# A transformer layer on one core: projections held back behind a stack load, GpSimd for the rows of the maxima, and weighting two key tiles behind the scores

## The reference, cut to what matters

```python
h = layernorm(x) * (1 + ca) + sa                   # ca, sa, ... from silu(c) @ wmod
qkv = h @ w_qkv.T + b_qkv                          # heads of width 16
scores = q @ k.T / 4 + causal                      # per head, 2048 x 2048
x = x + ga * ((softmax(scores) @ v) @ w_out.T + b_out)
h = layernorm(x) * (1 + cb) + sb
gate = h @ gate_weight.T                           # top-1 of 8 experts, 320 places each
x = x + gb * experts(h)                            # exact gelu, scatter and gather by rank
```

## Time and profile before

| what | value |
|---|---|
| three runs, us | 782.27, 780.64, 782.81; median 782.27 |
| profiled execution, us | 778.72 |
| its span, first to last instruction, us | 777.0 |
| mean granted TensorE clock | 0.927 of 2.4 GHz |
| PE busy | 676.4 us, 87% |
| DVE busy | 561.8 us, 72% |
| ACT busy | 455.8 us, 59% |
| POOL busy | 134.1 us, 17% |

### The profile page before, as it was taken

One profiled execution on the slowest core, in us unless ns is written; L12 is line 12 of the kernel. 1 busy time (PEld: TensorE's weight loads), 2 busy tenths in 40 slices (PEclk: granted clock), 3 DMA queues, 4 the chain that ended last, 5 costly groups with the idle time before them and its releaser, 6 DMA issues.

```text
span 777.0 us, 12195 instructions
## 1 busy us (share of the span) xinstructions
PE 676.4 (87%) x4290; PEld 370.4 (48%) x4290; DVE 561.8 (72%) x1467; ACT 455.8 (59%) x962; POOL 134.1 (17%) x194
## 2 busy tenths in 40 slices
PE   4686889489899999999999999988986279999994
PEld 3555444232333344333333333334533269999994
DVE  7763778468798987989998989974435447777762
ACT  1432546256577776777777777765761346666651
POOL 6000322130001122103221101100005300121122
PEclk9988889689899999999999999999987569999997
DMA  7435236531005123106800032000004283455200
GB/s 244 105 91 136 48 75 147 127 71 23 1 1 133 31 55 82 29 1 155 280 1 1 1 122 96 2 0 28 29 27 152 106 232 116 158 193 202 81 23 18
DMA packets 42111, 66.53 MB, mean 86 GB/s; under 512 B 3822, under 2 KB 31985, under 8 KB 41466
## 3 DMA queue, kind: packets, MB, share of 16 engines
q1 hardware_dynamic: 39746, 59.44, 27.3%
q0 software_dynamic: 2304, 6.31, 2.2%
HBM read 39.36 MB, written 26.78 MB: 85 GB/s over the span
## 4 chain that ended last, share of the span: by engine, by line
PE 69%; DVE 9%; issue 8%; ACT 7%; DMA 4%; POOL 1%; SPq 1%; DVEq 0%; POOLq 0%; ACTq 0%
PE bank L1280 15%; PE bank L1330 13%; PE bank L1358 13%; PE bank L1464 9%; PE bank L1447 8%; PE bank L1225 3%; ACT probs L842 3%; DMA qk_rows<-part 2%; PE bank L1383 2%; PE bank L1430 1%; DVE chunk_max L1089 1%; PE bank L1254 1%; PE bank L1407 1%; ACT stacks L831 1%; ACT qk_sb L792 1%
## 5 line engine op out<-in xcount | busy, mean ns | idle before, releaser
L842 ACT ACTIVATE probs<-bank 128x512 f32<-128x512 f32 (+3 forms) x640 | 295.2, 540 | 105.4 <-PE bank L1358 103.6
L1089 DVE TENSOR_REDUCE chunk_max<-bank 128x1 f32<-128x512 f32 x384 | 251.5, 685 | 30.4 <-PE bank L1330 28.7
L1358 PE MATMUL bank<-stacks 104*128 104x512 bf16 (+3 forms) x640 | 188.3, 358 | 19.6 <-DVE stacks L1115 12.3
L1330 PE MATMUL bank<-stacks 96*128 96x512 bf16 (+3 forms) x640 | 195.6, 359 | 7.1 <-DVE chunk_max L1089 4.0
L1280 PE MATMUL bank<-probs,v_sb 128*32 128x512 f32 (+3 forms) x1280 | 154.8, 557 | 0.4 <-POOL probs L738 0.4
L1095 DVE CUSTOM_DVE_ANT_0 masked<-bank,causal 128x128 bf16<-128x128 f32 (+3 forms) x256 | 120.7, 484 | 21.6 <-PE bank L1330 20.6
L1330 PEld LDWEIGHTS bank<-stacks 96*128 96x128 bf16 x640 | 55.6, 98 | 154.2 <-DVE chunk_max L1089 74.6
L738 POOL TENSOR_SCALAR_AFFINE_SELECT probs<-probs 128x512 f32<-128x512 f32 x64 | 40.8, 638 | 383.9 <-ACT probs L842 383.9
L1358 PEld LDWEIGHTS bank<-stacks 104*128 104x128 bf16 x640 | 63.1, 101 | 83.4 <-ACT probs L842 18.4
L1464 PE MATMUL bank<-w_split,acts 128*128 128x256 f32 x576 | 79.3, 283 | 0.0
L1464 PEld LDWEIGHTS bank<-w_split,acts 128*128 128x128 f32 x576 | 73.9, 189 | 1.5 <-issue 0.8
(11 more groups left out here) (140 smaller groups left out, 538.2 us busy)
## 6 DMA issues: line engine op xcount, KB each, us to landing
stacks<-qk_rows SPq DMA_DIRECT2D x6, 1536.0 KB, 12.2
w_raw<-w_in SPq DMA_DIRECT2D x8, 1024.0 KB, 5.0
w_raw<-w_down SPq DMA_DIRECT2D x8, 1024.0 KB, 8.1
qk_rows<-part SPq DMA_DIRECT2D x32, 192.0 KB, 2.8
slot_rows<-empty SPq DMA_DIRECT2D x1, 5140.0 KB, 28.9
slots_sb<-slot_rows SPq DMA_DIRECT2D x8, 514.0 KB, 4.2
qk_rows<-part SPq DMA_DIRECT2D x32, 128.0 KB, 2.4
stacks<-qk_rows SPq DMA_DIRECT2D x8, 384.0 KB, 4.3
```

What stands on the lines that cost most here:

```text
L842: act.activation(probs[:, s % 3, h, 0:width], of_ring(*ev)[:, 0:width], ACT.Exp)\
L1089: dve.tensor_reduce(to, src[:, 0:QB], AX.X, ALU.max).then_inc(max_read, 1)
L1330: pe.matmul(bank[MAX_BANKS[u % 3]][:, 0:width], stack(g, 0)[0:KR, h, q0:q0 + P], stack(g, 1)[0:KR, h, c * QB:c * QB + width], start=True, ...
L1358: pe.matmul(of_ring(*ev)[:, 0:QB - lo], stack(g, 1)[0:KR + MR, h, kt * P:(kt + 1) * P], stack(g, 0)[0:KR + MR, h, b * QB + lo:(b + 1) * QB ...
```

## The change

Three edits. First, the planner holds back a group's projections while the stacks of the group before are on their way: a new condition `stacks_on_way` asks that `STACK_TIME - SPLIT_TIME` (15000 of the planner's nanoseconds) have passed since `parts_at` of the group before. Second, from block n = 4 on (`PARTS_BY_POOL`), the split of the maxima and the copy of the rows to three heads run on GpSimd instead of VectorE; `neg_max` gets two buffers and a semaphore of its own, and the planner's costs for these steps are changed. Third, a key tile is weighted two tiles behind its scores (`WEIGH_LAG`) instead of one; the turn of the heads of the block before moves from the second to the third key tile, and its `heads_out` from the first to the second.

```diff
+PARTS_BY_POOL = NB
+WEIGH_LAG = 2
...
             plan.append(("max_parts", n))
-            vector[-1] += 400
-            waiting_rows.append([n, vector[-1] + 100])
+            vector[-1] += 640 if n < PARTS_BY_POOL else 220
+            waiting_rows.append([n, vector[-1] + 100 + (0 if n < PARTS_BY_POOL else 800)])
...
-            placed_at[n] = now + 1700
-            vector[-1] = max(vector[-1], now + 550) + 450
+            placed_at[n] = now + (1700 if n < PARTS_BY_POOL else 2700)
+            if n < PARTS_BY_POOL:
+                vector[-1] = max(vector[-1], now + 850) + 690
...
-        if projections and not split and block >= PROJECT_FROM[projections[0][0]] and now >= projected + SPLIT_TIME:
+        stacks_on_way = projections and now < parts_at.get(projections[0][0] - 1, 0.0) + STACK_TIME - SPLIT_TIME
+        if projections and not split and not stacks_on_way and block >= PROJECT_FROM[projections[0][0]] \
+                and now >= projected + SPLIT_TIME:
...
-                if may_go_beside(n, (i, h) > (1, 1)) and not (n == NG * NB - 1 and h == HG - 1):
+                if may_go_beside(n, (i, h) > (WEIGH_LAG, 1)) and not (n == NG * NB - 1 and h == HG - 1):
...
-                if h == 1 and n >= 1 and i == 1:
+                if h == 1 and n >= 1 and i == WEIGH_LAG:
                     plan.append(("turn_heads", n - 1))
...
-            if weigh is not None:
+            if len(weighings) == WEIGH_LAG:
+                weigh = weighings.pop(0)
                 fill(weigh[3])
                 plan.append(("weigh", weigh[0], weigh[1]))
                 tensor(HG * weigh[2] * 234 / QB, weigh[3])
-                if weigh[0] < n:
+                if weigh[0] < n and i == WEIGH_LAG - 1:
                     plan.append(("heads_out", n - 1))
...
     plan += beside
-    plan.append(("weigh", weigh[0], weigh[1]))
+    for weigh in weighings:
+        plan.append(("weigh", weigh[0], weigh[1]))
... on GpSimd
+                if ev[0] == "max_parts" and ev[1] >= PARTS_BY_POOL:
+                    pool.wait_ge(neg_max_known, n + 1)
+                    pool.wait_ge(ring_filled, turn_of["max_rows", n - 2] + 1)
+                    link(pool.tensor_copy(max_part[:, n % 2, :, 0], neg))
+                    pool.tensor_tensor(max_part[:, n % 2, :, 1], neg, max_part[:, n % 2, :, 0], ALU.subtract)\
+                        .then_inc(max_parts, 1)
+                if ev[0] == "max_rows" and ev[1] >= PARTS_BY_POOL:
+                    pool.wait_ge(diag_done, masked_tiles)
+                    if biased:
+                        pool.wait_ge(x_biased, biased)
+                    pool.wait_ge(rest_ready_p, n_rests)
+                    if n_parts:
+                        pool.wait_ge(qk_split_p, n_parts)
+                    pool.wait_ge(max_row0, n + 1)
+                    pool.tensor_copy(rows[:, 1:HG, :], rows[:, 0:1, :].broadcast_to([MR, HG - 1, QB]))\
+                        .then_inc(max_rows, 1)
+                    pool.wait_ge(max_rows, n + 1)
... on VectorE
                     if n >= 2:
+                        dve.wait_ge(max_parts, n - 1)
+                    neg = neg_max[:, n % 2, :]
+                    dve.tensor_reduce(neg, chunk_max[:, n % 2, :, 0:b + 1], AX.X, ALU.max, negate=True)\
+                       .then_inc(neg_max_known, 1)
+                    if n < PARTS_BY_POOL:
... the two operations of the split, as before
-                if ev[0] == "max_rows":
+                if ev[0] == "max_rows" and ev[1] < PARTS_BY_POOL:
```

More of the change, by code:

```diff
@@ L229, in project @@
                 parts_at[split[0]] = now + SPLIT_TIME
-    weigh = None
+    weighings = []
     beside = [ev for k in range(TAIL_TILES + TAIL_LAG + 1) for ev in tail_slot(k, 0, TAIL_TILES)]
@@ L275, in attention_plan @@
                 tensor(HG * weigh[2] * 234 / QB, weigh[3])
-                if weigh[0] < n:
+                if weigh[0] < n and i == WEIGH_LAG - 1:
                     plan.append(("heads_out", n - 1))
                     scalar = max(scalar, now + TO_READER) + 480
-            weigh = (n, kt, width, scalar + TO_WRITER + (MASK_TIME if kt >= b * TB else 0))
+            weighings.append((n, kt, width, scalar + TO_WRITER + (MASK_TIME if kt >= b * TB else 0)))
             project()
     plan += beside
-    plan.append(("weigh", weigh[0], weigh[1]))
-    plan.append(("heads_out", weigh[0]))
-    plan.append(("turn_heads", weigh[0]))
+    for weigh in weighings:
+        plan.append(("weigh", weigh[0], weigh[1]))
+    plan.append(("heads_out", NG * NB - 1))
+    plan.append(("turn_heads", NG * NB - 1))
     for k in range(TAIL_TILES, NT + TAIL_LAG + 1):
@@ L415, in layer @@
         chunk_max = sb1("chunk_max", [P, 2, TB * HG, NB], F32)
-        neg_max = sb1("neg_max", [P, TB * HG], F32)
+        neg_max = sb1("neg_max", [P, 2, TB * HG], F32)
         max_part = sb1("max_part", [P, 2, TB * HG, 2], BF16)
@@ L477, in layer @@
         max_parts = sem("max_parts")
+        neg_max_known = sem("neg_max_known")
         max_row0 = sem("max_row0")
@@ L722, in _ @@
             pool.memset(empty[:, ROW - 1:ROW].bitcast(I32), S).then_inc(empty_ready, 1)
-            biased = 0
+            biased = masked_tiles = n_rests = n_parts = 0
             for ev in plan:
@@ L727, in _ @@
                     leave_part0(pool, ev[1] * NB + ev[2], rest_ready_p)
+                    n_rests += 1
                 if ev[0] == "split":
                     leave_part1(pool, ev[1] * NB + ev[2], qk_split_p)
+                    n_parts += 1
+                if ev[0] == "max_parts" and ev[1] >= PARTS_BY_POOL:
+                    n = ev[1]
+                    neg = neg_max[:, n % 2, :]
[5 more added lines that the diff above has]
+                if ev[0] == "max_rows" and ev[1] >= PARTS_BY_POOL:
+                    n = ev[1]
+                    g, b = divmod(n, NB)
+                    rows = stack(g, 0)[KR:KR + MR, :, b * QB:(b + 1) * QB]
+                    pool.wait_ge(diag_done, masked_tiles)
[8 more added lines that the diff above has]
+                    pool.wait_ge(max_rows, n + 1)
                 if ev[0] == "scores" and ev[3] == HG - 1:
@@ L739, in _ @@
                                            pattern=[[0, HG], [1, P]], channel_multiplier=-1).then_inc(diag_done, 1)
+                        masked_tiles += 1
                     if j >= 0 and BIAS_FROM <= n and biased < NT:
@@ L1102, in _ @@
                     dve.wait_ge(max_read, units_before[n + 1])
-                    link(dve.tensor_reduce(neg_max[:, :], chunk_max[:, n % 2, :, 0:b + 1], AX.X, ALU.max, negate=True))
                     if n >= 2:
[L1105 to L1108, removed]
-                if ev[0] == "max_rows":
+                        dve.wait_ge(max_parts, n - 1)
+                    neg = neg_max[:, n % 2, :]
+                    dve.tensor_reduce(neg, chunk_max[:, n % 2, :, 0:b + 1], AX.X, ALU.max, negate=True)\
+                       .then_inc(neg_max_known, 1)
+                    if n < PARTS_BY_POOL:
+                        dve.wait_ge(neg_max_known, n + 1)
+                        if n >= 2:
+                            dve.wait_ge(ring_filled, turn_of["max_rows", n - 2] + 1)
+                        link(dve.tensor_copy(max_part[:, n % 2, :, 0], neg))
+                        dve.tensor_tensor(max_part[:, n % 2, :, 1], neg, max_part[:, n % 2, :, 0], ALU.subtract)\
+                            .then_inc(max_parts, 1)
+                if ev[0] == "max_rows" and ev[1] < PARTS_BY_POOL:
                     n = ev[1]
```

## The result

| | before | after |
|---|---|---|
| median us | 782.54 (4 runs, 780.64 to 784.18) | 758.75 (4 runs, 756.52 to 762.18) |
| ratio, 95% interval | 1 | 0.9701 [0.9657, 0.9744] |
| profiled execution, span us | 777.0 | 757.6 |
| mean granted clock of TensorE | 0.92 | 0.93 |

The forecast was 764.5, the measured median 758.75: 23.8 us faster where 18.0 were forecast. The profile after, view by view.

A forecast was written before the change was run, and what follows sets the result against it. TensorE was taken to bound 213 to 523 us, with a hole before block 2. Terms -9.6 - 2.7 - 5.0 + 1.5 + 1.5 - 1.2 + 1.2 - 3.5 = -17.8 took the 782.27 median to 764.5; forecast 761 to 769, range 756 to 775.

The forecast's parts named there:

- The stall: Before block 2's first score, TensorE waits behind stores queued after the load of group 1's stacks; its removal: -9.6 us.
- the second wait: At 157.36 us ScalarE waits again for stores and the next score waits 2.71 us; its removal: -2.7 us.
- Where the projection lands: Projection (2,0), held back by a later gate, moves by 11 to 15 us, to 138 to 142 us.
- Clock, -5.0 + 1.5: Half-speed work at 147 to 151 and 158 to 164.5 us goes, -5.0; possible half clock before block 2, +1.5.
- the prediction's own signs of being wrong: A wait on line 798 that stays, a 0.50 clock in block 2, or score matmuls waiting for rows in several blocks.
- the first rival: The wait before block 2 goes, but its run-up stays VectorE-bound and the clock falls anyway: about -10, 772 us; 17%.
- GpSimd's copy, 1.57 us and +1.2: Row copy on GpSimd takes 1.57 us, delaying scores in blocks 15 and 11, plus hand-over: +1.2 us.
- VectorE's relief, -1.2, at most -5.3: VectorE loses 13 us of work over 12 blocks, where TensorE's whole gap is 5.3: -1.2 us, bounds 0 and -5.3.
- The turned heads, -3.5: In block 15 a score's 3.68 us wait for the turned heads goes: -2.7, clock -0.8; bounds -5.2 and 0.
- what is late next: After the heads turn later, tile 5's output projection waits for VectorE to read tile 4's: some 1 us.
- The rival with 758 us: VectorE's relief is worth all of TensorE's gap, 5.3 instead of 1.2, and the heads 5.2: -24 us; 12%.

The follow-up runs named there:

- gate: The kernel before with the hold-back of the projections alone; 765.23 us, ratio 0.9816.
- gate_pool: The whole change without the lag, so the kernel before with the hold-back and GpSimd's part; 753.79 us, ratio 0.9659.
- gate_relief: The kernel before with the hold-back and GpSimd doing rows and splits from the fifth block on, in the order planned with the old times; 762.9 us, ratio 0.9765.
- late_lag: The whole change with the lag of two only from block 4 on, one before it; 751.23 us, ratio 0.9626.
- rank_later: The kernel before with only the ranking of the first 12 tiles put two heads' scores later; 777.09 us, ratio 0.9974.

## Why the prediction was right, and where it was not

- **The stall and the second wait, -12.3: right.** TensorE's idle time from 84 to 215 us fell from 21.4 to 10.0, by 11.4. No store meets the load, for the reason given. Alone, the hold-back with its clock measured -14.4 (interval -17.6 to -11.1), forecast -14.3.
- **Where the projection lands: wrong.** (2,0) was forecast at 138 to 142 us; ScalarE reads it at 150.15. The later load (132.32, not 126.93) accounts for 5.4 of that, and `gate`, with the load at 127.64 and no lag, has it at 144.32. No row shows a price for it.
- **Clock, -5.0 + 1.5: right in sense alone, wrong in the whole.** In `gate` 6.0 us of work run at half from 134.5 to 141.3 and none after, until block 15, for 16.3 us of work before from 137 to 203: -5.2. In the whole change 9.1 (136.2 to 146.4) and 6.1 (187.4 to 194.2) run at half: -0.5. A clock of 0.50 in block 2 was one of the prediction's own signs of being wrong, and it came; here the first rival, in which the run-up is bound by VectorE and the clock falls anyway, was nearer: from 134 to 139 us VectorE is busy 4.90 of 5.00 us and TensorE 3.42. The row that the term had left out was the half clock at the maxima of block 3: the sum let it stand as it was, and all four profiles with the hold-back and no lag in the first blocks (`gate`, `gate_pool`, `gate_relief`, `late_lag`) lose it, while all with the lag there keep 3.4 to 6.4 us of work at half. Why the lag lets TensorE wait longer just there was seen only in this pattern of waits, not taken apart.
- **GpSimd's copy, 1.57 us and +1.2: price right, weight too high.** It takes 1.46. In `gate_relief` the score behind it waits 1.34 us for 1.17 before: 0.2 more, forecast 0.9. In after, where the rows of block 15 are turned well ahead, no such wait is left. By the figure of the Trainium skill's GPSIMD Engine Reference, section 3.1 (1.8 cycles an element), it would have been an estimated 2.3; the run gives 1461 / 1536 = 0.95 ns an element, 1.1 cycles at the page's 1.2 GHz, so here the measurement decides against that figure. The page's other statement, about half of VectorE's speed, agrees with the trace (1461 ns against 703). With 2.3 the prediction's own steps give +2.6, not the +2.5 that it has.
- **VectorE's relief, -1.2, at most -5.3: the step that failed.** The argument was that TensorE has only 5.3 us of gaps from 213 to 523 us. That holds, and the gaps stay (283.31 of 287 us busy before, 283.28 after). But the sum costed only the work moved, and not the order that the planner makes from its new times. That order was a term put at nothing. In it the maxima end 16 to 20 us further ahead of block 15, and the gain falls behind block 14, outside the stretch that was argued about: 10.2 us from block 4 to the experts in `gate_pool`, 1.6 in `gate_relief`. Measured on top of the hold-back the part is worth 12.3 us (0.9816 to 0.9659), on top of hold-back and lag 6.9 (0.9789 to 0.9701, the intervals just touching).
- **The turned heads, -3.5: fair alone, nothing of it left in the whole.** One tile later gives -4.9 by itself, and "what is late next" was the output projection, 1.7 to 2.2 us where 1 was said. But the new order removes the same wait without the lag. So from block 4 to the experts the whole change gains no more than `gate_pool` (10.5 against 10.2), and the lag cost 3 to 7 us in the first blocks: from `gate_pool` to the whole change the ratio goes from 0.9659 to 0.9701, though these intervals overlap; the profiles and `late_lag` carry this point.
- **The sum: partly luck.** Its -17.8 came near the measured -23.4 (1 less the ratio, times 782.54) through errors of both signs: some 7 to 12 us missing for the order, and some 3 of clock plus 3.5 of turned heads too many. The rival with 758 us named nearly the measured time, but by a mechanism that is not the one found: it filled TensorE's gaps, which did not change.

## What to carry to other kernels

Where an order of work is planned from costs, a changed cost is a change of its own: plan both versions and compare where each event lands before pricing the work moved. A relieved engine that is not the bound can still pay where its backlog is drained at a change of phase, so look at what it still owes when the next phase begins. And test each part with and without the others: here hold-back and lag mended the same stall, order and lag the same wait, and the best kernel (751.23 us) leaves the lag out of the first blocks, where it costs.

## What the hardware showed that was not expected

The clock of the first 90 us differs between executions of the same instructions. `rank_later` changes nothing ahead of the last blocks, yet its profile has block 0's first exponential 4.9 us later than before, behind stretches at a lower granted clock. Windows of the kernel before, then of `rank_later`:

```profile
34.00:55.00 21.00, 15.05 (x64) 9.96 (x64) 13.50 (x51) 6.34 (x8) 0.00 (x0) 0.76 0.29 73
65.00:89.00 24.00, 18.57 (x100) 11.35 (x98) 13.85 (x40) 7.40 (x18) 2.43 (x3) 0.79 0.31 68
```

```profile
34.00:55.00 21.00, 15.82 (x58) 10.70 (x59) 12.78 (x50) 5.18 (x6) 0.00 (x0) 0.59 0.30 74
65.00:89.00 24.00, 17.62 (x67) 12.31 (x68) 10.93 (x31) 5.23 (x8) 0.64 (x1) 0.64 0.35 81
```

Ahead of that exponential 26.6 us of TensorE's work run at half in `rank_later` and 13.5 before; the difference costs some 6.5 us, enough for the 4.9. It is why single profiles differ by 5 us before the changed code is reached, and why the leads above are best read as differences from block 0 on. In one set of 17 runs of the kernel before, the mean clock lay between 0.914 and 0.931 and the time between 785.85 and 776.06 us, the shortest times at the highest clocks; so effects under some 3 us can't be told here from a few runs.
